# Attention over 4096 positions: products with V in runs of eight, two batches of ones instead of three

## The reference

```python
x_flat = x.reshape(B, C, H * W).transpose(0, 2, 1)
Q = split_heads(x_flat @ Wq + bq); K = split_heads(x_flat @ Wk + bk); V = split_heads(x_flat @ Wv + bv)
attn = softmax(einsum('bhnd,bhmd->bhnm', Q, K) * head_dim ** -0.5)
out = einsum('bhnm,bhmd->bhnd', attn, V)
out = out.transpose(0, 2, 1, 3).reshape(B, H * W, C) @ Wo + bo
y = out + x_flat
y = (y - mean(y)) / sqrt(var(y) + 1e-5) * gamma + beta
```

## Time and profile before

| what | value |
|---|---|
| median of 3 runs | 5707.13 us (5706.82 to 5709.15) |
| the profiled execution's own time | 5707.97 us |
| its span | 5706.1 us |
| TensorE matmul busy | 5383.5 us, 94% of the span, 26288 instructions |
| VectorE busy | 4962.4 us, 87%, 7348 instructions |
| ScalarE busy | 3795.9 us, 67%, 7385 instructions |
| GpSimd busy | 4202.1 us, 74%, 3277 instructions |
| transposes of the maxima (one per chunk) | 128, from 89.2 us to 3743.9 us |

### The profile page before, as it was taken

How to read it: one execution, slowest core, us unless ns; L and a number is a source line. 1 busy time by engine, 2 the same in 40 slices (tenths; PEclk the granted TensorE clock), 3 DMA queues, 4 the chain that set the end, 5 groups by cost and what they waited for, 6 DMA issues and landing times. The chain is left out here.

```text
span 5706.1 us, 83184 instructions
## 1 busy us (share of the span) xinstructions
PE 5383.5 (94%) x26288; PEld 2482.6 (44%) x26288; DVE 4962.4 (87%) x7348; ACT 3795.9 (67%) x7385; POOL 4202.1 (74%) x3277
## 2 busy tenths in 40 slices
PE   7999999999999999999999999978888888888888
PEld 3544444444444444444444444423333333333333
DVE  6888888888888888888888888838999999999999
ACT  3666666666666666666666666657777777777776
POOL 4777776677776677777667777646888888888887
PEclk8999999999999999999999999989999999999999
DMA  4111121211112211112111010125555555555555
GB/s 139 35 53 49 36 62 63 65 52 40 47 45 64 78 41 52 41 43 59 61 56 29 23 34 18 58 84 183 189 188 187 188 187 189 186 190 188 187 188 172
DMA packets 337480, 549.25 MB, mean 96 GB/s; under 512 B 76016, under 2 KB 99568, under 8 KB 335600
## 3 DMA queue, kind: packets, MB, share of 16 engines
q1 hardware_dynamic: 327536, 526.62, 28.7%
q10 hardware_dynamic: 9504, 17.31, 1.1%
HBM read 415.10 MB, written 109.84 MB: 92 GB/s over the span
## 5 line engine op out<-in xcount | busy, mean ns | idle before, releaser
L625 DVE TENSOR_REDUCE mpart<-ps 128x1 f32<-128x512 f32 x4096 | 2536.8, 680 | 572.4 <-PE ps L400 568.7
L526 ACT ACTIVATE exps<-ps 128x512 f32<-128x512 f32 x4096 | 2124.1, 602 | 1251.8 <-PE ps L407 1250.0
L602 POOL TENSOR_TENSOR sums<-exps 128x512 f32<-128x512 f32 x1408 | 1789.9, 1292 | 527.0 <-ACT exps L526 524.5
L400 PE MATMUL ps<-k_st,q_ring 96*128 96x512 f32 x4096 | 1746.1, 428 | 19.1 <-DMA k_st<-qk_split 14.6
L407 PE MATMUL ps<-q_ring,k_st 98*128 98x512 f32 x4096 | 1620.3, 397 | 4.0 <-ACT exps L526 3.6
L1284 POOL TENSOR_TENSOR hc<-hh,c_rep 128x512 f32<-128x512 f32 x1024 | 1294.7, 1277 | 312.3 <-DVE hh L1253 293.0
L1253 DVE TENSOR_TENSOR_SCAN hh<-d_a,carry,ps 128x512 f32<-128x512 f32 x1024 | 1289.6, 1262 | 0.0
L400 PEld LDWEIGHTS ps<-k_st,q_ring 96*128 96x128 f32 x4096 | 774.9, 189 | 1066.8 <-DVE mpart L625 593.3
L602 POOL TENSOR_TENSOR held<-exps 128x512 f32<-128x512 f32 x640 | 815.9, 1296 | 531.2 <-ACT exps L526 531.2
L418 PE MATMUL ps<-exps,v_ring 128*32 128x512 f32 x8192 | 1090.9, 605 | 0.0
L407 PEld LDWEIGHTS ps<-q_ring,k_st 98*128 98x128 f32 x4096 | 778.2, 190 | 142.7 <-ACT exps L526 17.3
(11 more groups left out here) (111 smaller groups left out, 3363.7 us busy)
## 6 DMA issues: line engine op xcount, KB each, us to landing
d_a<-dt_dram SPq DMA_DIRECT2D x1040, 256.0 KB
qk_split<-hilo SPq DMA_DIRECT2D x128, 256.0 KB, 2.3
out_dram<-out_sb SPq DMA_DIRECT2D x128, 256.0 KB, 2.0
heads_in<-out_dram SPq DMA_DIRECT2D x32, 1024.0 KB, 5.3
q_ring<-qk_split SPq DMA_DIRECT2D x384, 64.0 KB, 2.0
k_st<-qk_split SPq DMA_DIRECT2D x45, 512.0 KB, 7.1
dt_dram<-dt SPq DMA_DIRECT2D x33, 512.0 KB, 5.5
s_u<-lo_u ACTq DMA_DIRECT2D x66, 256.0 KB, 6.6
```

Of the source, the lines that this page charges most:

```text
L400: nc.tensor.matmul(d_bank(("max", m, t)), q_ring[0:PARTS, m % 4, 128 * i:128 * i + 128], k_st[0:PARTS, g % 2, chunk(kc)], start=True, stop ...
L526: nc.scalar.activation(exps[:, u % EXPS, CH * half:CH * half + CH], a_bank(("exp", n, t)), ACT.Exp, scale=SCALE).then_inc(a_done, 1)
L602: pool.tensor_tensor(dst, exps[:, u % EXPS, 0:CH], exps[:, u % EXPS, CH:2 * CH], ALU.add).then_inc(summed, 1)
L625: nc.vector.tensor_reduce(mpart[:, m % 2, t % 4, t // 4:t // 4 + 1], d_bank(("max", m, t)), AX.X, ALU.max).then_inc(d_done, 1)
```

## The change

The products with V are issued for two groups at once, behind 16 score tiles (after groups 0, 2, 4 and 6, for the two groups before). The order of score tiles in a group alternates: M M E M E M E E in odd groups, M E M E E M E M in even ones. Six pair sums are held instead of five, and VectorE joins them in three pieces, one after group 4 and two after group 6. Of the ten other pairs, GpSimd merges 6 with 7, 8 with 9 and 12 with 13 by one more addition each, over a new tile `second`. That leaves seven units and the held one, so eight, in two batches of ones: behind the products of groups 4 and 5, and of 6 and 7. The copy of the denominators moves from VectorE to ScalarE, to between the exponentials of groups 1 and 2.

```diff
-HELD = 5
-ALONE = PAIRS - HELD
-UNITS = ALONE + 1
+HELD = 6
+FIRSTS, SECONDS, SINGLES = (6, 8, 12), (7, 9, 13), (10, 11, 14, 15)
+UNIT_OF = {6: 0, 8: 1, 10: 2, 11: 3, 12: 4, 14: 5, 15: 6}
+UNITS = len(UNIT_OF) + 1
+POOL_SUMS = PAIRS + len(SECONDS)
+PIECES = ((0, 176), (176, 344), (344, 512))
 def units(u):
-    return {4: (5, 6, 7, 8), 6: (9, 10, 11, 12), 7: (13, 14, 15, None)}.get(u, ())
+    return {5: (0, 1, 2, 3), 7: (4, 5, 6, 7)}.get(u, ())
+def pool_sums(u):
+    return u + 1 + sum(1 for w in SECONDS if w < u)
...
                 def sum_exps(n, v):
-                    if v == 4 and n:
+                    if v == 5 and n:
                         pe.wait_ge(den_read, n)
-                    pe.wait_ge(summed, n * PAIRS + (2 * v + 1 if v < 7 else PAIRS))
-                    for j, u in enumerate(units(v)):
...
+                    pe.wait_ge(summed, n * POOL_SUMS + pool_sums(11 if v == 5 else 15))
+                    for j, k in enumerate(units(v)):
...
                     for v in range(QUADS):
-                        for i in range(4):
-                            for m, t in max_tiles(n, v)[i:i + 1]:
-                                max_tile(m, t)
-                            for m, t in exp_tiles(n, v)[i:i + 1]:
-                                exp_tile(m, t)
+                        maxima, exponentials = max_tiles(n, v), exp_tiles(n, v)
+                        for step in ("MMEMEMEE", "MEMEEMEM")[(v + 1) % 2]:
+                            if step == "M":
+                                for m, t in maxima[:1]:
+                                    max_tile(m, t)
+                                maxima = maxima[1:]
+                            else:
+                                for m, t in exponentials[:1]:
+                                    exp_tile(m, t)
+                                exponentials = exponentials[1:]
...
                         m, u = (n, v - 1) if v else (n - 1, QUADS - 1)
-                        if 0 <= m < NS:
+                        if 0 <= m < NS and u % 2:
+                            attn_v(m, u - 1)
                             attn_v(m, u)
...
+                def read_den(n):
+                    act.wait_ge(sum_used, n * UNITS + UNITS)
+                    if n >= 2:
+                        act.wait_ge(den_stored[n % 2], 16 * (n // 2))
+                    nc.scalar.copy(den_parts[:, n % 2, :], ps[:, DEN_BANK, :]).then_inc(den_read, 1)
...
                         if v == 0 and 0 <= n - 1 < NS:
                             read_out(n - 1)
+                        if v == 1 and 0 <= n - 1 < NS:
+                            read_den(n - 1)
...
                         if n:
-                            pool.wait_ge(joined, 4 * n)
+                            pool.wait_ge(joined, len(PIECES) * n)
                         dst = held[:, :, u]
+                    elif u in SECONDS:
+                        pool.wait_ge(summed, n * POOL_SUMS + pool_sums(u - 1))
+                        dst = second[:, :]
...
                     pool.tensor_tensor(dst, exps[:, u % EXPS, 0:CH], exps[:, u % EXPS, CH:2 * CH], ALU.add).then_inc(summed, 1)
+                    if u in SECONDS:
+                        unit = sums[:, (n * (UNITS - 1) + UNIT_OF[u - 1]) % 8, :]
+                        pool.wait_ge(summed, n * POOL_SUMS + pool_sums(u - 1) + 1)
+                        pool.tensor_tensor(unit, unit, second[:, :], ALU.add).then_inc(summed, 1)
...
-                    a = slice(128 * i, 128 * i + 128)
+                    a = slice(*PIECES[i])
                     nc.vector.tensor_reduce(held_sum[:, a], held[:, a, :], AX.X, ALU.add).then_inc(joined, 1)
...
                             if 0 <= n + 1 < NS:
                                 shift_rows(n + 1)
-                            if 0 <= n - 1 < NS:
-                                read_den(n - 1)
-                        if v in (3, 4, 5, 6) and 0 <= n < NS:
-                            join_held(n, v - 3)
+                        if 0 <= n < NS:
+                            if v == 4:
+                                join_held(n, 0)
+                            if v == 6:
+                                join_held(n, 1)
+                                join_held(n, 2)
```

More of the change, by code:

```diff
@@ L171, in layer0 @@
         held_sum = sb("held_sum", [128, CH])
+        second = sb("second", [128, CH])
         out_sb = sb("out_sb", [128, 2, CH])
@@ L424, in sum_exps @@
                 def sum_exps(n, v):
-                    if v == 4 and n:
+                    if v == 5 and n:
                         pe.wait_ge(den_read, n)
-                    pe.wait_ge(summed, n * PAIRS + (2 * v + 1 if v < 7 else PAIRS))
-                    for j, u in enumerate(units(v)):
-                        if u is None:
-                            pe.wait_ge(joined, 4 * n + 4)
-                        part = held_sum[:, :] if u is None else sums[:, (n * ALONE + u - HELD) % 8, :]
+                    pe.wait_ge(summed, n * POOL_SUMS + pool_sums(11 if v == 5 else 15))
+                    for j, k in enumerate(units(v)):
+                        if k == UNITS - 1:
+                            pe.wait_ge(joined, len(PIECES) * (n + 1))
+                        part = held_sum[:, :] if k == UNITS - 1 else sums[:, (n * (UNITS - 1) + k) % 8, :]
                         nc.tensor.matmul(ps[D * j:D * j + D, DEN_BANK, :], ones_d[:, :], part,
-                                         start=(v == 4), stop=(v == QUADS - 1)).then_inc(sum_used, 1)
+                                         start=(v == 5), stop=(v == QUADS - 1)).then_inc(sum_used, 1)
                 def turn_max(m):
@@ L524, in exp_tile @@
                         act.wait_ge(av_done, n * PAIRS + u - EXPS + 1)
-                        act.wait_ge(summed, n * PAIRS + u - EXPS + 1)
+                        m, w = divmod(n * PAIRS + u - EXPS, PAIRS)
+                        act.wait_ge(summed, m * POOL_SUMS + pool_sums(w))
                     nc.scalar.activation(exps[:, u % EXPS, CH * half:CH * half + CH], a_bank(("exp", n, t)), ACT.Exp, scale=SCALE
@@ L594, in pair_sum @@
                         if n:
-                            pool.wait_ge(joined, 4 * n)
+                            pool.wait_ge(joined, len(PIECES) * n)
                         dst = held[:, :, u]
+                    elif u in SECONDS:
+                        pool.wait_ge(summed, n * POOL_SUMS + pool_sums(u - 1))
+                        dst = second[:, :]
                     else:
-                        i = n * ALONE + u - HELD
+                        i = n * (UNITS - 1) + UNIT_OF[u]
                         if i >= 8:
-                            pool.wait_ge(sum_used, (i - 8) // ALONE * UNITS + (i - 8) % ALONE + 1)
+                            pool.wait_ge(sum_used, (i - 8) // (UNITS - 1) * UNITS + (i - 8) % (UNITS - 1) + 1)
                         dst = sums[:, i % 8, :]
                     pool.tensor_tensor(dst, exps[:, u % EXPS, 0:CH], exps[:, u % EXPS, CH:2 * CH], ALU.add).then_inc(summed, 1)
+                    if u in SECONDS:
+                        unit = sums[:, (n * (UNITS - 1) + UNIT_OF[u - 1]) % 8, :]
+                        pool.wait_ge(summed, n * POOL_SUMS + pool_sums(u - 1) + 1)
+                        pool.tensor_tensor(unit, unit, second[:, :], ALU.add).then_inc(summed, 1)
                 def low(p, i):
@@ L630, in join_max @@
                     nc.vector.tensor_reduce(mneg[:, m % 2, :], mpart[:, m % 2, :, :], AX.X, ALU.max, negate=True).then_inc(mneg_ready, 1)
[L632 to L636, removed]
                 def shift_rows(m):
@@ L649, in join_held @@
                     if i == 0:
-                        dve.wait_ge(summed, n * PAIRS + HELD)
+                        dve.wait_ge(summed, n * POOL_SUMS + HELD)
                         if n:
                             dve.wait_ge(sum_used, n * UNITS)
-                    a = slice(128 * i, 128 * i + 128)
+                    a = slice(*PIECES[i])
                     nc.vector.tensor_reduce(held_sum[:, a], held[:, a, :], AX.X, ALU.add).then_inc(joined, 1)
```

## The result

The changed kernel takes 5796.27 us (median of 4 runs, 5794.15 to 5798.57) against 5706.98 (4 runs): ratio 1.0156, 95% interval 1.0138 to 1.0173. The prediction said 5720 with 5650 to 5790: the right side, six times too small, and the time is outside the range.

What follows compares the result with a forecast made beforehand. TensorE was taken to set the pace. Plain chunks -8, projection +12 and finish +11 us gave +15 on 5707.97: 5722, rounded 5720, range 5650 to 5790; the saving went into bank waits, the denominators' copy and GpSimd.

Steps and rivals of the forecast that it cites:

- What is taken off TensorE: Four there-and-back changes of kind and one batch of ones fewer on TensorE: 2.1 us per chunk, 269 us if all.
- The banks: Three PSUM banks each for maxima and exponentials: sixteen scores wait for reads, losing 0.37 us, 4.00 instead of 3.63.
- A: Run of sixteen scores of groups 7 and 0 in a chunk, with ones: 7.06 us.
- B: Run of sixteen scores of groups 1 and 2, with the transpose and ScalarE's denominators' copy mid-run: 6.68 us.
- C: Run of sixteen scores of groups 3 and 4 in a plain chunk: 6.2 us.
- The wait w: TensorE's ones in the run of groups 5 and 6 wait for GpSimd's pair 11: 0.2 to 0.4, taken as 0.3 us.
- each so costs 0.06 + 0.03 to 0.08 over the spacing: GpSimd's four additions that wait for its own last result: 0.36 to 0.56 us extra in all before pair 11 ends.
- My third rival: GpSimd's own-result waits are 0.3 us each instead of 0.12, TensorE's wait 1.0 in 101 chunks: 5793 us; chance 0.15.
- The finish chunks' waits: ScalarE's extra passes mid-run delay scores in chunks that finish: 32.4 us a chunk, slower by 0.4, +11 us.
- The first (all in time): GpSimd is in time for the ones and ScalarE's extra passes vanish into the runs: 5675 or 5650 us; chance 0.27.
- second (no bank waits): The PSUM banks don't bind at all: 25.2 us a chunk, 5464 us; chance 0.05.
- the fourth: Every product batch on TensorE pays its return, joined or not: +61 us, 5781 us; chance 0.05.

Runs made afterwards that it cites:

- The merges alone: Changed kernel with products again behind every eight scores in the old order, keeping GpSimd's merges and two batches of ones: 5597.4 us, 0.9805 times before.
- the runs alone: Changed kernel without GpSimd's merges: products in runs of eight and new score order kept, five held sums, three batches of ones: 5829.8 us, 1.0211 times before.
- the loosened wait: Changed kernel, but GpSimd's additions into `second` wait only for the merge that last read it, not the sum before: 5762.6 us, 1.0093 times before.

## Why the prediction was wrong

- **What is taken off TensorE** was right in size: products 0.88 apart in a run, and one batch of ones less. The merges alone give 1.0 us per chunk back, which I had only as a part of 2.1. Joining the heads in the middle of a run pays its return, as said: 1.00 us to the next score, where 0.86 led to the ones before.
- **The banks** were right to 0.03 us per run: A 7.06, B 6.70, C 6.22 against 7.06, 6.68 and 6.2. That the large saving ends there is shown by the runs alone (27.86 us for 27.86 worked out). VectorE did not bind, as said.
- **The wait w failed.** The step "each so costs 0.06 + 0.03 to 0.08 over the spacing" took its price from ScalarE's row; GpSimd pays 0.19 twice and 0.12 twice, 0.64 in all (unrounded) where the step gives 0.36 to 0.56 and the sum went by about 0.47. The second price in w, 0.05 from the sum to the ones, was taken from a load that waits for a bank; it is 0.15. Together w is 0.61 in plain chunks instead of 0.3 (some 24 us over the 77), and 0.84 in projection chunks instead of 0.6 (6 us over the 24; 4 more there lie outside w and were not traced). The mechanism was right and its size half of what it is. My third rival had this mechanism, with its price too high and a chance of 0.15.
- **The finish chunks' waits** were about right: without the slow stretch 32.62 against 32.4 (the extras, 31.97 less 27.43, are 4.5 and not 4.6). The sum's 77, 24 and 27 chunks are 72, 22 and 25 clean ones and 7 mixed. But no step had the granted clock, and this is the step that failed most: the sum put it at nothing. Eighteen times 1.61 us, 29 us, is the largest piece that I missed. The earlier trace rows showed 1.00 through the layer, and I carried that to a kernel whose TensorE waits.
- Together: 15 forecast, 24 + 6 for w, 4 for the projection chunks' rest, 29 for the clock, 5 for the finish chunks' rest, 5 after the last transpose (some 3 of them the two slow stretches there): 88 of the 89 us measured.
- **The rivals.** The first (all in time) and second (no bank waits) are excluded by the rows above, the fourth by the products' 1.92 us for eight: two batches that each paid a return would take 2.0.

## What to carry to other kernels

Before a longer run of one kind of work is built to save changes of kind, count the run against its buffers: with three banks and readers slower than the writer, sixteen tiles lost here what four changes saved, and what a reader does mid-run comes on top: 0.70 of the affine pass's 0.83 us, 0.16 of the copy's 0.48. Take the two parts of a change apart: here one part was worth -110 us, and the other, which alone costs 122 us, cost 199 on top of it, mostly by a wait that a plain chunk has with neither part alone. And price an engine's wait for its own result from that engine.

## What was not expected of the hardware

- GpSimd's additions of 128 x 512 float32 that wait for its own last result follow at 1.36 us (merge) and 1.43 (into `second`), those that wait for nothing at 1.24; the loosened wait took the additions into `second` back to 1.25. Why the two differ wasn't tried.
- In a layer in which TensorE is otherwise full, one exposed wait (a score 0.85 us behind the one before it) and a 16-row matmul close behind it were followed by the 1.2 GHz level for the eight products after them (3.1 to 3.6 us instead of 1.9), or part of them, in 18 of 25 full finish chunks. With the products between the two it stayed at 2.4 GHz in all 25, and without the wait as well. Why seven chunks with the same rows stayed at the higher level is open; in the runs without the merges, with the same wait, 15 did.
